# Four output additions of the shared expert ahead of the group selection, and new call orders on all five engines

## The chip, the cores and the metric

The kernel runs on one core of a Trainium2 chip. The metric is the device time of one execution in microseconds (us), the median of several runs; lower is better. The engines are TensorE (PE, its weight loads PEld), VectorE (DVE), ScalarE (ACT), GpSimd (POOL) and SyncE (SP), which issues most of the DMA.

## What is computed

```python
xn = _layernorm(x)
x = x + _L0_attn_ref(xn, Wq, Wk, Wv, Wo) + _L0_ffn_ref(xn, ...)
# attention: x is (2, 512, 512), 32 heads of 128 over 8 key heads, rope, causal
scores = jnp.einsum('bkgtd,bksd->bkgts', qg, k) * scale
attn = jax.nn.softmax(jnp.where(causal, scores, -jnp.inf), axis=-1)
out = jnp.einsum('bkgts,bksd->bkgtd', attn, v)        # then times Wo
# ffn: 16 experts in 4 groups; the best 2 groups, in them the best 2 experts
scores = softmax(xt @ router_w + router_b) + router_bias
keep = top 2 groups by their largest score; idx = top 2 experts in them
y = sum over chosen e of gate_e * (silu(xt @ w1 + b1) * (xt @ w2 + b2)) @ w3 + b3
z = silu(xt @ sw1 + sb1) * (xt @ sw2 + sb2) @ sw3 + sb3   # shared expert
```

## The kernel before

All products of weights and of attention run as three fp32r matmuls, since each operand is split into a high part and the rest (`*_hi`, `*_lo`). The high part is written by ScalarE or GpSimd (a copy to fp32r), the rest by VectorE or GpSimd (a subtraction).

**Front.** The rows are normalised, transposed, routed; the shared expert's two halves give 8 row blocks of 128 tokens each. TensorE computes `down(n)` for each block into four banks (`DOWN_BANKS`), VectorE adds it to the sum `y` (`add_down(n)`, line 1310). Four blocks are of batch 0 and four of batch 1, and `down` of one bank can only start again when VectorE has added what was in it. VectorE also does the routing: group selection (lines 1340 to 1346), then the first largest expert twice (`first_largest`, lines 1330 to 1334), `chosen`, and the gates. The key and value projection of head 0 and its queries follow on TensorE.

**Heads.** There are 8 key heads g. Head 0 is `first_head`, heads 1 to 6 run as a hardware loop over `key_head`, head 7 is `last_head`. Each of the five engines has the three functions as a plain list of calls, one per piece of work, and walks it in order; semaphores alone tie the engines together. A head holds, for each batch b and row block i: `scores` (TensorE), `maxima` (VectorE, the row maxima, line 1474), `exps` (ScalarE, line 876), `normalise` (GpSimd, line 636), `transpose_p` (TensorE), the split of the transposed probabilities (`lo_pT`, line 1502), `values` (TensorE), the split of its result (`lo_oT`, line 1487), `project_out` (TensorE) and `add_out` (VectorE). In between stand the next batch's or head's `project_kv` and `project_q`, whose results VectorE turns (`turn_k`, `turn_q1`, `turn_q2`) and GpSimd sums (`add_k`, `add_q`), and the transposition of k (`transpose_k`), whose bank must be read by `lo_kT` (line 1465) before `project_q(g, b, 2, 0)` may write it:

```python
if h < 2:
    pe.wait_ge(v_split, count(2, g, b, h + 1))
elif h == 2:
    pe.wait_ge(kT_split, count(1, g, b, 1))
```

**Experts.** Each head also carries five of the 31 expert tiles of 128 rows (`tile_of(g, m)`, 5g + m - 5; calls with a tile or head out of range do nothing). Head 0 computes the places of the rows (`first_places(0, k)` on VectorE: `count_blocks`, `first_blocks`, `row_slots`, `row_gates`, `experts_of_tiles`, lines 1370 and on) and GpSimd scatters them with indirect DMAs (`place_x`, line 645). Head 7 gathers the results (`collect`) and VectorE adds them in four steps (`combine_two(g, i)`, four instructions each on line 1586).

Of the kernel before, what the change touches and what calls it, by code (L numbers as in the profile page):

```python
# [17 lines left out]
TB = T // P  # L18
# [89 lines left out]
def build(nc, x, wq, wkv, wo, shared, sb3, w12, w3, b12, b3, router_w, router_b, router_bias,  # L108
# [8 lines left out]
    with ExitStack() as ctx:  # L117
# [167 lines left out]
        def _(sp):  # L285
# [103 lines left out]
            def first_head(g):  # L389
                e4 = load_x(tile_of(g, 4))  # L390
                load_wo(g, 1)
                e2 = load_x(tile_of(g, 2))
                load_wo(g, 3)
                e1 = load_x(tile_of(g, 1))
                e3 = load_x(tile_of(g, 3))
                load_b12(tile_of(g, 1), e1)
                load_b12(tile_of(g, 3), e3)
                load_wo(g, 2)
                load_b12(tile_of(g, 2), e2)
                load_wo(g, 0)  # L400
# [10 lines left out]
                load_wkv(g)  # L411
                load_wq(g, 1)
                store_y(tile_of(g, 0))
                store_y(tile_of(g, 3))
                load_wq(g, 2)
                load_w3(tile_of(g, 1), e1)
                load_wq(g, 3)
                load_b3(tile_of(g, 1), e1)
# [4 lines left out]
                load_b3(tile_of(g, 4), e4)  # L423
                load_b12(tile_of(g, 5), e5)
                load_w3(tile_of(g, 5), e5)
                load_b12(tile_of(g, 4), e4)
                load_b3(tile_of(g, 5), e5)
                load_w12(tile_of(g, 1), e1)

            def key_head(g):  # L430
                e1 = load_x(tile_of(g, 1))
                load_b12(tile_of(g, 1), e1)
                load_w12(tile_of(g, 1), e1)
                load_wo(g, 0)
                load_w3(tile_of(g, 1), e1)
                load_wq(g, 0)
                load_wo(g, 1)
                load_wo(g, 2)
                load_wo(g, 3)
                load_wkv(g)  # L440
                store_y(tile_of(g, 0))
                e2 = load_x(tile_of(g, 2))
                load_b3(tile_of(g, 1), e1)
                load_b12(tile_of(g, 2), e2)
                load_w12(tile_of(g, 2), e2)
                load_wq(g, 1)
                load_w3(tile_of(g, 2), e2)
                store_y(tile_of(g, 1))
                load_wq(g, 2)
                e3 = load_x(tile_of(g, 3))  # L450
                load_w12(tile_of(g, 3), e3)
                load_b3(tile_of(g, 2), e2)
                load_w3(tile_of(g, 3), e3)
                store_y(tile_of(g, 2))
                load_b12(tile_of(g, 3), e3)
                e4 = load_x(tile_of(g, 4))
                load_wq(g, 3)
                load_w12(tile_of(g, 4), e4)
                load_b3(tile_of(g, 3), e3)
                store_y(tile_of(g, 3))  # L460
                load_w3(tile_of(g, 4), e4)
                e5 = load_x(tile_of(g, 5))
                load_b12(tile_of(g, 4), e4)
                load_b3(tile_of(g, 4), e4)
                load_w12(tile_of(g, 5), e5)
                store_y(tile_of(g, 4))
                load_w3(tile_of(g, 5), e5)
                load_b12(tile_of(g, 5), e5)
                load_b3(tile_of(g, 5), e5)

            def last_head(g):
                load_wq(g, 0)
                e1 = load_x(tile_of(g, 1))
                load_wq(g, 2)
                e4 = load_x(tile_of(g, 4))
                store_y(tile_of(g, 2))
                load_w12(tile_of(g, 1), e1)
                e3 = load_x(tile_of(g, 3))
                e5 = load_x(tile_of(g, 5))
                e2 = load_x(tile_of(g, 2))  # L480
                load_wq(g, 1)
                load_b3(tile_of(g, 4), e4)
                load_w3(tile_of(g, 2), e2)
                load_b12(tile_of(g, 1), e1)
                load_b12(tile_of(g, 5), e5)
                load_b12(tile_of(g, 4), e4)
                load_wq(g, 3)
                load_b3(tile_of(g, 3), e3)
                load_wo(g, 0)
                load_w12(tile_of(g, 2), e2)  # L490
                load_wo(g, 1)
                load_w12(tile_of(g, 5), e5)
                load_b3(tile_of(g, 1), e1)
                store_y(tile_of(g, 1))
                load_b12(tile_of(g, 3), e3)
                store_y(tile_of(g, 3))
                load_wkv(g)
                load_w3(tile_of(g, 1), e1)
                load_w12(tile_of(g, 4), e4)
                load_w3(tile_of(g, 4), e4)  # L500
                load_w12(tile_of(g, 3), e3)
                store_y(tile_of(g, 0))
                load_b3(tile_of(g, 2), e2)
                load_w3(tile_of(g, 5), e5)
                load_wo(g, 3)
                store_y(tile_of(g, 4))
                load_b12(tile_of(g, 2), e2)
                load_wo(g, 2)
                load_b3(tile_of(g, 5), e5)
                load_w3(tile_of(g, 3), e3)  # L510
# [14 lines left out]
        def _(pool):  # L525
# [160 lines left out]
            def first_head(g):  # L686
# [3 lines left out]
                normalise(g, 0, 1)  # L690
                normalise(g, 0, 2)
                add_k(g, 1, 1)
                add_q(g, 1, 1)
                place_x(g, 0)
# [3 lines left out]
                collect(g, 1)  # L698
                add_q(g, 1, 3)
                split_q(g + 1, 0)  # L700
                collect(g, 2)
                split_q(g + 1, 1)
                normalise(g, 1, 0)
                collect(g, 3)
                place_x(g, 1)
                normalise(g, 1, 1)
                add_k(g + 1, 0, 0)
                place_x(g, 2)
                add_q(g + 1, 0, 0)
                add_k(g + 1, 0, 1)  # L710
                split_q(g + 1, 2)
                normalise(g, 1, 2)
# [4 lines left out]
                collect(g, 0)  # L717
                add_q(g + 1, 0, 3)

            def key_head(g):  # L720
                lo_w12(tile_of(g, 0))
                add_k(g, 1, 0)
# [3 lines left out]
                collect(g, 2)  # L726
                add_q(g, 1, 0)
                lo_w3(tile_of(g, 1))
                lo_w12(tile_of(g, 1))
                add_k(g, 1, 1)  # L730
                normalise(g, 0, 2)
                add_q(g, 1, 1)
                split_kv(g + 1)
                collect(g, 3)
                lo_w12(tile_of(g, 2))
                split_q(g + 1, 0)
# [3 lines left out]
                add_q(g, 1, 3)  # L740
                lo_w3(tile_of(g, 2))
                normalise(g, 1, 0)
                split_q(g + 1, 1)
                split_q(g + 1, 2)
                lo_w12(tile_of(g, 3))
                add_q(g + 1, 0, 0)
                collect(g, 0)
                add_k(g + 1, 0, 0)
                normalise(g, 1, 1)
                lo_w3(tile_of(g, 3))  # L750
                lo_w12(tile_of(g, 4))
                normalise(g, 1, 2)
                place_x(g, 2)
                place_x(g, 1)
                add_k(g + 1, 0, 1)
                add_q(g + 1, 0, 1)
                split_q(g + 1, 3)
                add_q(g + 1, 0, 2)
                lo_w3(tile_of(g, 4))
                normalise(g, 1, 3)  # L760
                add_q(g + 1, 0, 3)
                collect(g, 1)

            def last_head(g):
                add_k(g, 1, 0)
                lo_w3(tile_of(g, 0))
                place_x(g, 2)
                normalise(g, 0, 0)
                lo_w12(tile_of(g, 0))
                normalise(g, 0, 1)  # L770
                add_q(g, 1, 0)
                normalise(g, 0, 2)
                add_k(g, 1, 1)
                place_x(g, 1)
                add_q(g, 1, 1)
                normalise(g, 0, 3)
                add_q(g, 1, 2)
                collect(g, 0)
# [6 lines left out]
                place_x(g, 0)  # L785
                normalise(g, 1, 1)
                normalise(g, 1, 0)

# [6 lines left out]
        def _(act):  # L795
# [161 lines left out]
            def first_head(g):  # L957
                exps(g, 0, 0, 0)
                hi_wo(g, 0)
                exps(g, 0, 0, 1)  # L960
                hi_wo(g, 1)
# [249 lines left out]
        def _(dve):  # L1211
# [125 lines left out]
            for n in range(2):  # L1337
                add_down(n)
# [9 lines left out]
            for n in range(2, TB):  # L1348
                add_down(n)
# [1449 lines left out]
```

How the kernel before makes its waits and increments, by code:

```python
def wait_count(eng, sem, value):  # L51
    if not isinstance(value, int) or value > 0:
        eng.wait_ge(sem, value)
# [229 lines left out]
        @block.sync  # L284
# [18 lines left out]
            for h in range(G):  # L303
                sp.dma_start(wq_raw[:, h, :], wq[h]).then_inc(wq_in[h], 16)
            sp.dma_start(qc[:, :], q_cos).then_inc(tables_in, 16)
            sp.dma_start(qs[:, :], q_sin).then_inc(tables_in, 16)
            sp.dma_start(kr[:, :, :, :], k_rot).then_inc(tables_in, 16)
            sp.wait_ge(zeros_ok, 1)
            for n0, n1 in ZERO_PARTS:
                sp.dma_start(x_slots[P * n0:P * n1, :].rearrange("(p n) (m d) -> p (n m) d", p=P, m=2),
# [5 lines left out]
            def load_wq(g, h):  # L316
                if no_head(g + 1):
                    return
                sp.wait_ge(q_psum, count(4, g, 1, h + 1))
                sp.dma_start(wq_raw[:, h, :], row(wq, G * g + (G + h))).then_inc(wq_in[h], 16)
# [1 line left out]
            def load_wkv(g):  # L323
                if no_head(g + 1):
                    return
                sp.wait_ge(kv_psum, count(2, g, 1, 2))
                sp.dma_start(wkv_raw[:, :, :, :].rearrange("p c k o -> p (c k o)"),
                             wkv[bass.ds(g + 1, 1), :, :, :, :].rearrange("a p c k o -> (a p) (c k o)")).then_inc(wkv_in, 16)
# [1 line left out]
            def load_wo(g, c):  # L331
                if isinstance(g, int) and g == 0:
                    sp.wait_ge(down_psum, NB)
                else:
                    sp.wait_ge(o_psum, 32 * g + (c - 3))
# [873 lines left out]
        @block.vector  # L1210
# [197 lines left out]
            dve.wait_ge(tables_in, 48)
```

## Time and profile before

| | |
|---|---|
| median of 3 runs | 907.06 us (906.69 to 907.95) |
| profiled execution, its own time | 905.59 us |
| its span | 903.8 us |
| PE busy | 888.5 us, 98% of the span |
| PEld busy | 762.2 us, 84% |
| DVE busy | 677.7 us, 75% |
| ACT busy | 431.2 us, 48% |
| POOL busy | 526.5 us, 58% |
| granted TensorE clock | full in every fortieth of the span |
| moved by DMA | 97.73 MB, mean 108 GB/s |

TensorE is busy almost throughout. Its matmuls overlap, so a row's duration is longer than the distance to the next: 128x512 matmuls of one stream start 0.23 us apart. What a wait costs is therefore read as the distance between two starts less that 0.23 us. The 1.8 us between span and own time lie around the program.

### The profile page before, as it was taken

The numbers are of one execution on the slowest core, as the hardware profiler recorded it, in microseconds if no ns is written. First come the engines' busy times: TensorE is split into PE (matmuls) and PEld (weight loads), VectorE is DVE, ScalarE is ACT, GpSimd is POOL, SyncE is SP. The second block draws the span as 40 slices with busy tenths as digits, with TensorE's granted clock in tenths as the row PEclk, the third lists the DMA queues.
The fourth block names the chain that finished last, engine by engine and source line by source line (L and its number), as shares of the span: only waits on it lengthen the run. The fifth ranks groups of instructions, "written<-read, shape, count | busy, mean of one in ns | idle before, by whom it ended". The sixth has DMA issues, their size and how long they took to land.

```text
span 903.8 us, 17478 instructions
## 1 busy us (share of the span) xinstructions
PE 888.5 (98%) x5066; PEld 762.2 (84%) x5066; DVE 677.7 (75%) x1614; ACT 431.2 (48%) x1083; POOL 526.5 (58%) x638
## 2 busy tenths in 40 slices
PE   8997999999999999999999999999999999999998
PEld 7786887888888888888888889888888888888886
DVE  6688876687767876768767786768776787676886
ACT  3504543554535644454554545445453564454543
POOL 5923786565654765538554575356565476543663
PEclk9999999999999999999999999999999999999999
DMA  9910223143223532335222443224322252230242
GB/s 329 319 47 15 92 94 123 42 131 121 88 76 86 172 95 79 90 99 168 87 87 76 114 163 87 75 81 126 123 87 75 89 172 94 80 92 22 84 150 94
DMA packets 52161, 97.73 MB, mean 108 GB/s; under 512 B 5920, under 2 KB 17824, under 8 KB 52128
## 3 DMA queue, kind: packets, MB, share of 16 engines
q1 hardware_dynamic: 49568, 88.94, 31.7%
q0 software_dynamic: 2560, 8.39, 2.8%
q8 instruction: 16, 0.26, 0.1%
q14 instruction: 17, 0.14, 0.1%
HBM read 74.76 MB, written 22.54 MB: 108 GB/s over the span
## 4 chain that ended last, share of the span: by engine, by line
PE 92%; DVE 5%; issue 1%; ACT 1%; DMA 0%; POOL 0%; SPq 0%; DVEq 0%
PE bank L1992 10%; PE bank L1990 10%; PE bank L1991 10%; PE bank L2190 7%; PE bank L2129 7%; PE bank L2131 6%; PE bank L2130 6%; PE bank L2226 6%; PE bank L2222 6%; PE bank L2223 6%; PE bank L2206 4%; PE bank L2203 4%; PE bank L2204 4%; PE bank L2251 1%; PE bank L2176 1%
## 5 line engine op out<-in xcount | busy, mean ns | idle before, releaser
L636 POOL TENSOR_SCALAR prob<-prob,rsum 128x128 f32<-128x128 f32 (+3 forms) x256 | 143.9, 582 | 89.8 <-DVE rsum L1480 89.1
L876 ACT ACTIVATE prob<-bank,nmax 128x128 f32<-128x128 f32 (+3 forms) x256 | 133.7, 528 | 113.9 <-DVE nmax L1474 111.3
L1474 DVE CUSTOM_DVE_ANT_0 bank<-bank,causal 128x128 f32<-128x128 f32 (+3 forms) x256 | 122.8, 501 | 35.5 <-PE bank L1992 33.7
L1502 DVE TENSOR_TENSOR pT_lo<-bank,pT_hi 128x512 fp32r<-128x512 f32 x160 | 109.1, 684 | 29.0 <-ACT pT_hi L896 28.6
L896 ACT ACTIVATE pT_hi<-bank 128x512 fp32r<-128x512 f32 x160 | 95.0, 596 | 67.1 <-PE bank L2190 53.4
L2222 PE MATMUL bank<-wo_lo,oT_hi 128*128 128x512 f32 x256 | 106.2, 415 | 0.0
L2129 PE MATMUL bank<-xT_hi,wq_lo 128*128 128x512 f32 x256 | 104.7, 409 | 1.5 <-DVE v_lo L1458 1.4
L619 POOL TENSOR_TENSOR w_lo<-w_raw,w_hi 128x1024 fp32r<-128x1024 f32 x31 | 74.3, 2398 | 52.7 <-ACT w_hi L931 52.7
L2131 PE MATMUL bank<-xT_hi,wq_hi 128*128 128x512 f32 x256 | 101.1, 395 | 0.0
L2226 PE MATMUL bank<-wo_hi,oT_lo 128*128 128x512 f32 x256 | 100.7, 393 | 0.0
L2130 PE MATMUL bank<-xT_lo,wq_hi 128*128 128x512 f32 x256 | 100.6, 393 | 0.0
L2223 PE MATMUL bank<-wo_hi,oT_hi 128*128 128x512 f32 x256 | 100.5, 392 | 0.0
L585 POOL TENSOR_TENSOR q_first<-rot 128x128 f32<-128x128 f32 x60 | 28.3, 472 | 115.3 <-DVE rot L1430 115.1
L2190 PE MATMUL bank<-ident,prob 128*128 128x128 f32 x640 | 94.1, 272 | 0.0
L2190 PEld LDWEIGHTS bank<-ident,prob 128*128 128x128 f32 x640 | 77.7, 140 | 13.5
L1990 PE MATMUL bank<-wkv_hi,xT_lo 128*128 128x256 f32 x256 | 74.7, 292 | 1.1 <-DVE prob L1430 0.8
L1992 PE MATMUL bank<-wkv_hi,xT_hi 128*128 128x256 f32 x256 | 72.3, 282 | 0.0
L1991 PE MATMUL bank<-wkv_lo,xT_hi 128*128 128x256 f32 x256 | 71.9, 281 | 0.0
L1990 PE MATMUL bank<-kT_hi,q_lo 128*128 128x256 f32 (+2 forms) x192 | 68.0, 354 | 3.1 <-ACT prob L876 2.9
L887 ACT ACTIVATE oT_hi<-bank 128x512 fp32r<-128x512 f32 x64 | 38.1, 595 | 65.9 <-PE bank L2206 65.2
L2203 PE MATMUL bank<-pT_hi,v_lo 128*128 128x512 f32 x160 | 65.5, 409 | 0.5 <-DVE oT_lo L1487 0.5
L1991 PE MATMUL bank<-kT_lo,q_hi 128*128 128x256 f32 (+2 forms) x192 | 64.7, 337 | 0.0
(219 smaller groups left out, 2326.5 us busy)
## 6 DMA issues: line engine op xcount, KB each, us to landing
w_raw<-w SPq DMA_DIRECT2D x31, 512.0 KB, 3.5
wq_raw<-wq SPq DMA_DIRECT2D x32, 256.0 KB, 4.1
wo_raw<-wo SPq DMA_DIRECT2D x32, 256.0 KB, 2.8
xg<-x_slots SPq DMA_DIRECT2D x31, 256.0 KB, 3.5
w_raw<-w SPq DMA_DIRECT2D x31, 256.0 KB, 2.8
eb<-b SPq DMA_DIRECT2D x31, 256.0 KB, 3.9
y_slots<-eb SPq DMA_DIRECT2D x31, 256.0 KB, 2.5
x_slots<-pairs SPq DMA_DIRECT2D x3, 2048.0 KB, 16.0
```

The lines of the kernel that those rows point to most:

```text
L636: last = nc.gpsimd.tensor_scalar(row, row, rsum[:, stat(b, i, h)], 1.0, ALU.mult, ALU.mult)
L876: last = nc.scalar.activation(prob[n % 2][:, h, 0:P * (i + 1)], bank[S_BANKS[use % 2]][:, 256 * k:256 * k + P * (i + 1)], ACT.Exp, bias=nm ...
L1990: nc.tensor.matmul(dst, a_lo, c_hi, start=start and k == 0, stop=False)
L1991: nc.tensor.matmul(dst, a_hi, c_lo, start=False, stop=False)
L1992: last = nc.tensor.matmul(dst, a_hi, c_hi, start=False, stop=stop and k == len(terms) - 1)
L2129: nc.tensor.matmul(q, wq_lo[:, h, col], xT_hi[:, c, span], start=c == 0, stop=False)
L2130: nc.tensor.matmul(q, wq_hi[:, h, col], xT_lo[:, c, span], start=False, stop=False)
L2131: last = nc.tensor.matmul(q, wq_hi[:, h, col], xT_hi[:, c, span], start=False, stop=c == HC - 1)
L2190: last = nc.tensor.transpose(bank[PT_BANKS[n % 2]][:, h * P:(h + 1) * P], prob[nth(g, b, i) % 2][:, h, j * P:(j + 1) * P], ident[:, :])
L2222: nc.tensor.matmul(dst, oT_hi[:, k, h], wo_lo[:, h, :], start=h == 0, stop=False)
L2223: nc.tensor.matmul(dst, oT_hi[:, k, h], wo_hi[:, h, :], start=False, stop=False)
L2226: last = nc.tensor.matmul(dst, oT_lo[:, k, h], wo_hi[:, h, :], start=False, stop=h == G - 1)
```

## The change

Two things change. First, VectorE does the first four `add_down` ahead of the group selection, where it did two there and two behind the group masks. Second, the lists of calls `first_head`, `key_head` and `last_head` of all five engines are put in another order. Every list has the same calls for real heads and tiles as before; no instruction is added or taken away, and no tile changes its size. Behind the two removed lines all line numbers are lower by 2.

```diff
             hidden(3)
-            for n in range(2):
+            for n in range(TB):
                 add_down(n)
             in_groups = score.rearrange("p n (g e) -> p n g e", g=GROUPS)
...
             nc.vector.tensor_tensor(masked_groups, masked_groups, ...)
-            for n in range(2, TB):
-                add_down(n)
             spare, one, two = (pick[:, k] for k in range(3))
```

A line or two of the lists, from VectorE's `last_head`:

```diff
                 lo_pT(g, 1, 2, 0)
+                lo_pT(g, 1, 2, 1)
                 combine_two(g, 2)
+                lo_pT(g, 1, 2, 2)
                 inverse_sums(g, 1, 1)
-                lo_pT(g, 1, 2, 1)
-                lo_pT(g, 1, 2, 2)
                 maxima(g, 1, 0, 0)
                 maxima(g, 1, 0, 1)
                 lo_oT(g, 1, 2)
                 combine_two(g, 3)
+                lo_pT(g, 1, 1, 0)
                 inverse_sums(g, 1, 0)
-                lo_pT(g, 1, 1, 0)
                 lo_pT(g, 1, 1, 1)
```

On TensorE in `last_head`, `project_out(g, 1, 3, 0)` moves ahead of `values(g, 1, 2, 0)`, and `values(g, 1, 2, 1)` now follows that directly, where a projection, a transposition and two scores lay between. On GpSimd in `first_head`, `place_x(g, 0)` moves from behind `normalise(g, 0, 2)`, `add_k(g, 1, 1)` and `add_q(g, 1, 1)` to ahead of them, and `place_x(g, 2)` from ahead of `add_q(g + 1, 0, 0)` to behind it.

**VectorE in the front**, from the end of the shared expert's hidden rows (`hid`, `h_lo`) over the additions (line 1310) to the start of the group selection, and then the end of the group masks:

```order
 L1261 SCALAR_TENSOR_TENSOR hid<-bank,eraw,act_out 128x512
 L1265 TENSOR_TENSOR h_lo<-hid,h_hi 128x512
-L1310 TENSOR_TENSOR y<-y,bank 128x512 x2
+L1310 TENSOR_TENSOR y<-y,bank 128x512 x4
 L1340 TENSOR_REDUCE grp<-route 128x32
 L1319 TENSOR_TENSOR beat<-grp 128x128
```

The four additions stand together; the two that are gone from behind the masks stood between the last mask instruction (line 1346) and the first of `first_largest` (line 1330).

**VectorE at the start of head 0**, the maxima of row block 0 (ISA, `nmax`) and the first step of the row places (lines 1370 to 1378 before, 1368 to 1376 now). Before:

```order
L1436 TENSOR_TENSOR q_lo<-prob,q_hi 128x384
L1474 ISA bank,nmax<-bank,causal 128x128
L1474 ISA nmax 128x1
L1474 ISA bank,nmax<-bank,causal 128x128
L1474 ISA nmax 128x1
L1370 TENSOR_REDUCE iota<-before 128x16
L1371 TENSOR_SCALAR iota<-iota 128x16
L1372 TENSOR_SCALAR per_expert<-iota 128x8
L1376 TENSOR_TENSOR pairs<-bank,per_expert 128x128
L1378 TENSOR_REDUCE per_expert<-pairs 128x16
```

and now:

```order
L1434 TENSOR_TENSOR q_lo<-prob,q_hi 128x384
L1368 TENSOR_REDUCE iota<-before 128x16
L1369 TENSOR_SCALAR iota<-iota 128x16
L1370 TENSOR_SCALAR per_expert<-iota 128x8
L1374 TENSOR_TENSOR pairs<-bank,per_expert 128x128
L1376 TENSOR_REDUCE per_expert<-pairs 128x16
L1472 ISA bank,nmax<-bank,causal 128x128
L1472 ISA nmax 128x1
```

`count_blocks`, the five instructions on 128x16 and the like, has moved from behind the first `maxima` call to ahead of it.

**VectorE in the loop**, in batch 0's last scores of each head, where `wo_lo` is `lo_wo(g, 2)`, `h_rows` the end of `expert_hidden`, and `kT_lo` is `lo_kT(g, 1)`. Before:

```order
L1562 SCALAR_TENSOR_TENSOR h_rows<-sig,gated 128x128
L1470 REGISTER_ALU
L1474 ISA bank,nmax<-bank,causal 128x512
L1474 ISA nmax 128x1
L1527 TENSOR_TENSOR wo_lo<-wo_raw,wo_hi 128x512
L1464 ISA
L1465 TENSOR_TENSOR kT_lo<-bank,kT_hi 128x512
```

and now:

```order
L1525 TENSOR_TENSOR wo_lo<-wo_raw,wo_hi 128x512
L1560 SCALAR_TENSOR_TENSOR h_rows<-sig,gated 128x128
L1468 REGISTER_ALU
L1472 ISA bank,nmax<-bank,causal 128x512
L1472 ISA nmax 128x1
L1462 ISA
L1463 TENSOR_TENSOR kT_lo<-bank,kT_hi 128x512
```

The subtraction of `wo_lo` has moved from directly ahead of `kT_lo` to ahead of `h_rows` and the maxima.

## Rows read from the trace of the kernel before

**Rows 1.** Busy time in stretches: stretch, length, each engine's busy us, PE clock, DMA

```profile
70.00:92.00 22.00, 17.44 (x121) 14.59 (x120) 18.37 (x62) 10.64 (x31) 9.23 (x15) 1.00 0.12 37
...
271.00:378.00 107.00, 107.00 (x625) 93.07 (x624) 80.05 (x193) 54.12 (x137) 62.45 (x74) 1.00 0.34 104
...
860.00:904.00 44.00, 39.65 (x206) 31.79 (x204) 34.43 (x75) 17.33 (x48) 21.14 (x28) 1.00 0.40 120
```

**Rows 2.** Waits of PE: line, released by, us in total, times, longest

```profile
PE bank L1990 <- ACT prob L876: 2.9, 4, 1.0
...
PE bank L2129 <- DVE v_lo L1458: 1.4, 2, 1.1
...
PE bank L2206 <- DVE pT_lo L1502: 0.5, 2, 0.4
```

**Rows 3.** Timeline of PE in the front: start, duration, idle before and releaser

```profile
48.57 0.40 PE L1992 MATMUL bank<-ew_hi,h_hi 128*128 128x512 f32 x1
49.96 0.50 PE L1990 MATMUL bank<-ew_hi,h_lo 128*128 128x512 f32 x1 [0.98 <-DVE y L1310]
```

**Rows 4.** Timeline of DVE, the additions and the turning of q

```profile
49.22 1.28 DVE L1310 TENSOR_TENSOR y<-y,bank 128x512 f32<-128x512 f32 x2
...
61.60 0.69 DVE L1422 TENSOR_TENSOR rot<-bank,qc 128x512 f32<-128x512 f32 x1 [1.09 <-PE bank L2131]
```

**Rows 5.** Timeline of DVE at the start of head 0

```profile
76.31 0.41 DVE L1370 TENSOR_REDUCE iota<-before 128x16 f32<-128x256 f32 x1
...
78.00 0.30 DVE L1474 CUSTOM_DVE_ANT_0 bank<-bank,causal 128x128 f32<-128x128 f32 x1 [0.23 <-DVE per_expert L1378]
```

**Rows 6.** Timeline of ACT at the start of head 0

```profile
75.36 1.28 ACT L876 ACT_TABLE_LOAD   x1
76.65 0.37 ACT L876 ACTIVATE prob<-bank,nmax 128x128 f32<-128x128 f32 x1
```

**Rows 7.** Timeline of POOL, PE and DVE in head 0, 129 to 144 us

```profile
129.34 0.97 POOL L645 DMA_INDIRECT x_slots<-xn,slots  x1 [0.30 <-issue]
130.04 0.34 PE L1992 MATMUL bank<-kT_hi,q_hi 128*128 128x384 f32 x1
...
131.56 0.57 DVE L1474 CUSTOM_DVE_ANT_0 bank<-bank,causal 128x384 f32<-128x384 f32 x1 [2.21 <-PE bank L1992]
...
143.45 0.48 PE L2129 MATMUL bank<-xT_hi,wq_lo 128*128 128x512 f32 x1 [1.11 <-DVE v_lo L1458]
```

**Rows 8.** Waits of PEld in the loop, 164 to 806 us

```profile
PEld bank L2129 <- DVE kT_lo L1465: 2.7, 6, 0.5
```

**Rows 9.** Timeline of all engines around `kT_lo` in the first loop head

```profile
202.14 1.01 DVE L1527 TENSOR_TENSOR wo_lo<-wo_raw,wo_hi 128x512 fp32r<-128x512 f32 x1
...
202.58 1.06 POOL L545 TENSOR_SCALAR wkv_hi<-wkv_raw 128x512 fp32r<-128x512 f32 x1
...
203.08 0.68 DVE L1465 TENSOR_TENSOR kT_lo<-bank,kT_hi 128x512 fp32r<-128x512 f32 x1
...
203.31 0.40 PE L2226 MATMUL bank<-wo_hi,oT_lo 128*128 128x512 f32 x1
...
203.81 0.50 PE L2129 MATMUL bank<-xT_hi,wq_lo 128*128 128x512 f32 x1
```

**Rows 10.** Line 1527: count, duration ns least/median/most, first and last start

```profile
L1527 DVE TENSOR_TENSOR wo_lo<-wo_raw,wo_hi x32: 673/684/1011, 92.8 to 853.9; 128x512 fp32r<-128x512 f32 x32
```

**Rows 11.** Timeline of PE in head 0, transpositions of k and the next q matmul

```profile
149.80 0.60 PE L2159 MATMUL bank<-ident,ksum 128*128 128x128 f32 x4
...
152.07 0.47 PE L2129 MATMUL bank<-xT_hi,wq_lo 128*128 128x512 f32 x1
```

**Rows 12.** Timeline of DVE and PE in head 7, a combining step and what follows

```profile
888.12 3.12 DVE L1586 SCALAR_TENSOR_TENSOR y<-gath,slot_gate,y 128x512 f32<-128x512 f32 x4
...
891.34 0.39 PE L2204 MATMUL bank<-pT_hi,v_hi 128*128 128x512 f32 x1
...
892.08 0.50 PE L2206 MATMUL bank<-pT_lo,v_hi 128*128 128x512 f32 x1 [0.35 <-DVE pT_lo L1502]
```

More of the change, by code:

```diff
@@ L2310, in first_head @@
                 scores(g, 0, 3, 1)
-                scores(g, 0, 3, 2)
                 project_q(g, 1, 1, 3)
                 project_out(g, 0, 0, 0)
-                values(g, 0, 1, 0)
+                scores(g, 0, 3, 2)
                 scores(g, 0, 3, 3)
@@ L2665, in last_head @@
                 transpose_p(g, 0, 3, 3)
+                scores(g, 1, 1, 0)
+                transpose_h(tile_of(g, 2))
                 values(g, 0, 3, 1)
+                scores(g, 1, 1, 1)
+                project_out(g, 0, 2, 1)
+                values(g, 0, 3, 2)
+                transpose_p(g, 1, 0, 0)
+                expert_down(tile_of(g, 2))
+                project_q(g + 1, 0, 0, 0)
+                values(g, 0, 3, 3)
+                project_q(g + 1, 0, 0, 1)
+                transpose_x(tile_of(g, 3))
@@ new lines, in key_head @@
+                project_out(g, 0, 2, 2)
+                project_q(g + 1, 0, 0, 2)
+                scores(g, 1, 2, 0)
+                project_q(g + 1, 0, 0, 3)
+                first_ranks(g)
+                project_out(g, 0, 2, 3)
+                scores(g, 1, 2, 1)
+                expert_up(tile_of(g, 3))
+                project_kv(g + 1, 0, 1, 0)
+                scores(g, 1, 2, 2)
+                scores(g, 1, 2, 3)
+                project_kv(g + 1, 0, 1, 1)
+                project_out(g, 0, 3, 0)
@@ new lines, in key_head @@
+                project_out(g, 0, 3, 1)
+                values(g, 1, 0, 0)
+                transpose_p(g, 1, 1, 0)
+                project_out(g, 0, 3, 2)
+                transpose_p(g, 1, 1, 1)
+                project_out(g, 0, 3, 3)
+                scores(g, 1, 3, 0)
+                transpose_h(tile_of(g, 3))
+                project_q(g + 1, 0, 1, 0)
+                scores(g, 1, 3, 1)
+                project_q(g + 1, 0, 1, 1)
+                project_out(g, 1, 0, 0)
+                scores(g, 1, 3, 2)
@@ new lines, in key_head @@
+                project_q(g + 1, 0, 1, 2)
+                project_q(g + 1, 0, 1, 3)
+                project_out(g, 1, 0, 1)
+                expert_down(tile_of(g, 3))
+                values(g, 1, 1, 0)
+                project_out(g, 1, 0, 2)
+                transpose_p(g, 1, 2, 0)
+                transpose_k(g + 1, 0)
+                scores(g, 1, 3, 3)
+                transpose_x(tile_of(g, 4))
+                project_out(g, 1, 0, 3)
+                project_q(g + 1, 0, 2, 0)
+                values(g, 1, 1, 1)
```

1515 lines of the change are left out of this document (733 added, 782 removed).

## The prediction

> **What bounds the kernel now.** I read the busy time by stretches first. In a head of the loop TensorE is busy for the whole 107.00 us at full clock, VectorE for 80, ScalarE for 54, GpSimd for 62, and the DMA share is a third [rows 1]. So TensorE's stream is the bound, the change neither adds nor removes a matmul, and all that an order can give is TensorE's waiting. The ends have some of that: from 70 to 92 us TensorE is busy 17.44 of 22.00, and from 860 to 904 us 39.65 of 44.00, where the last additions and the last store behind the final matmul take most of the rest [rows 1]. Second I read the list of TensorE's waits: the dearest that an order could touch are four for the exponentials, 2.9 us in all, two for `v_lo`, 1.4 us, and two for `pT_lo`, 0.5 us [rows 2]. The front's wait for an addition is in the timeline [rows 3]. Third, since a busy mark hides short gaps of a pipelined engine, I read the waits of the weight loads in the loop: six for `kT_lo`, 0.5 us each [rows 8], once per head and found in no matmul's idle time. There is nothing large: everything together is some 7 us, and each term below is at most 1.8.
>
> **The change part by part.** The sum is made against the profiled execution's own 905.59 us, which is 1.47 below the median shown, 907.06; I carry that difference over at the end.
>
> *The additions, front.* `down` of the seventh block starts at 49.96 where its predecessor started at 48.57, and the stream's pitch is 0.23: 49.96 - 48.57 - 0.23 = 1.16 us lost. The bank is free only once the third addition is done, and that stands behind the whole group selection, at 49.22 [rows 3, 4]. With four additions together the last is done some 4 x 0.64 = 2.6 us (two take 1.28) behind the start of the first, well before 48.57. The group selection starts 1.3 us later and ends where it ends now, because two additions are gone from its end: its chain stays as it is. The question is whether the 1.16 us reach the later work. The turning of the first queries starts at 61.60 after 1.09 us of waiting for TensorE [rows 4], so VectorE has that much room there. Term: -1.1 us, bounds -1.16 and 0 (if the routing chain alone set the start of head 0).
>
> *The first step of the row places, head 0.* `count_blocks` takes from 76.31 to 78.00, 1.69 us [rows 5], and now stands ahead of the first maxima, which were done at 76.31. Their exponential ran at 76.65, right behind the table load [rows 6], and would now come behind 78.0. The next maxima, which started at 78.00, move only by the 0.5 us or so of the call put between. TensorE already waits for exponentials in this stretch (the four waits of [rows 2] are mostly here), so each delay goes straight into its stream until the queries' projection, which takes one further wait away from it. I get 0.3 us on the second use, 0.4 to 0.5 on the later ones. Term: +0.5 us; bounds 0, and 78.0 - 76.65 = 1.35.
>
> The rows give the load as 1.28 us and the next activation 1.29 us behind its start. The Trainium skill, "ScalarE: Activation LUTs", What ACT_TABLE_LOAD costs, puts a drain of about 1380 ns on top, 2.66 us in all. By that page the exponential could not start before about 78.0 in either order, and putting `count_blocks` first would be free, the whole sum then 0.5 us lower; the row contradicts it here, since the activation starts at 76.65, and the sum goes by the row.
>
> *Row scatters, head 0.* Two results of TensorE are taken up late while GpSimd issues indirect DMAs: matmuls that started at 130.04 and take 0.34 are followed by the maxima at 131.56, 1.2 us late, and a `v_lo` later on costs TensorE 1.11 us at 143.45 [rows 7]. One of the four waits for exponentials follows from the first (2.9 / 4, some 0.7 us). What makes the signal late the rows don't say; it happens beside the scatters and not in every one. The scatters of blocks 0 and 1 move ahead of three calls, the last ones behind one, so other matmuls end beside them. I take -0.5 us, as if one of the two waits were missed half of the time more than one is found anew; bounds -1.8 (both gone) and +1.0 (one more).
>
> *The loop.* In each head `project_q(g, 1, 2, 0)` starts 203.81 - 203.31 = 0.50 behind its predecessor, 0.27 more than the pitch, and its weight load had waited for `kT_lo` [rows 8, 9]. `kT_lo` stands behind `wo_lo`, which here takes 1.01 us against 0.684 in the median [rows 9, 10], while GpSimd writes to SBUF beside it [rows 9]. With `wo_lo` ahead of `expert_hidden` and the maxima, `kT_lo` can start at about 202.2 and end at 202.9. TensorE has one 0.23 us matmul group fewer between the transposition and that projection by the order, about 0.4 us, so it wants `kT_lo` at 203.1: enough. The gain is 6 x 0.27 = 1.6 us at most. I take -1.2, since the many other calls that moved may put back a short gap; bounds -1.6 and 0.
>
> *The last head.* `values` at 892.08 starts 0.74 behind its predecessor, 0.51 more than the pitch, for a `pT_lo` that stands behind a 3.12 us combining step [rows 12]. The other `pT_lo` wait [rows 2] is 0.5 - 0.35 = 0.15 of idle, and with the same 0.16 for the restart 0.3. In the new lists one `pT_lo` more stands ahead of each of the last two combining steps. TensorE then asks for the second `pT_lo` earlier, so a piece of the gain at 892 may be paid at the step before. Term: -0.9 (both, and a little where a restart is saved in the same way); bounds -1.2 and 0.
>
> Sum: -1.1 + 0.5 - 0.5 - 1.2 - 0.9 = -3.2 us, 902.4 by its own time. With 1.47 for the median: **903.9 us**, 0.35% faster. A measurement of this kernel can tell about 0.2%, 1.8 us, from no change, so the border of faster is 905.25, that of slower 908.87.
>
> **The rivals.**
>
> *It comes out the same (0.24).* The front's 1.1 us is real, but head 0 is short of exponentials and eats it: +1.35 at the first places, the scatters' late signals as they are, and the loop's wait replaced by another of the same size, since in 107 us of new order any call may come just too early. -1.1 + 1.35 + 0 - 0.5 (loop) - 0.5 (last head) = -0.75: 906.3. For it: 98% busy leaves nothing that a reordering surely wins. Against it: the loop's wait has a plain cause that is plainly moved.
>
> *A new wait in the loop, slower (0.14).* Everything there counts six times. The tightest spot that I find by the order is `kT_lo(g + 1, 0)`: between the transpositions of k and the q matmul that waits for it TensorE's starts will now lie about 2.3 us apart, where by the order it was 3.0. In head 0 the same pair lay 152.07 - 149.80 = 2.3 apart and ran without a wait [rows 11]; but there VectorE had nothing else to do, and now an addition and a maxima call stand ahead. If these are just behind, each head loses up to their 0.7 + 0.7 us. It decides from 0.64 us per head, since (1.8 + 3.2 - 1.2) / 6 = 0.64; at 0.8 the loop adds 4.8 in place of its -1.2, and the sum is -2.0 + 4.8 = +2.8: 909.9. Against it: DVE is busy 80 of 107, and a late call catches up at once.
>
> *More than I take (in the likeliest case's lower part).* Both late signals gone and no loss at the first places: -1.1 - 1.8 - 1.6 - 1.2 = -5.7, 901.4.
>
> *The orders do nothing, only the additions count* lies in the first rival: -1.1, 906.0.
>
> **How the numbers follow.** Likeliest case 0.62, 903.9, its own range 902.0 to 905.3: its ends are one of the larger bounds (the scatters' or the loop's) going the other way. Same 0.24, 905.3 to 907.8. Slower 0.14, 908.9 to 912. The range 902.0 to 908.2 leaves out about 0.05 below and 0.13 above. Faster by over 0.2% 0.61, within 0.25, slower 0.14.
>
> **What would show it.** In the new profile: the gap ahead of the seventh block's `down`, at about 48.8, is gone and the first scores start 1.1 us earlier. The exponential behind the table load starts near 78 instead of 76.65, at unchanged length of the load. The list of weight-load waits in the loop has no `kT_lo`, and the distance between two heads is 0.27 us shorter; a longer one tells of the slower rival, and the row of waits names its call. GpSimd's scatters have late takers or not, to be read as idle time of VectorE ahead of `maxima` or `krot` of over 1 us behind a finished matmul. In the last head the `pT_lo` waits are gone. The forecast is wrong above all if the exponentials of head 0 hold up TensorE by more than 1 us in sum, or if a loop head grows.

## The result: slower by 1.6%, and the profile after

The changed kernel takes 921.68 us in the median of 4 runs (918.85 to 924.25), the kernel before 907.23 us beside it: a ratio of 1.0158, interval 1.0124 to 1.0192, 14.5 us slower. The prediction said 903.9, in a range of 902.0 to 908.2. The profiled execution took 924.25 us at a span of 922.5, so the sums below, which are made against it and the 903.8 us span of before, have 18.7 us to find.

Busy time by stretches of the changed kernel, columns as in [rows 1]:

```profile
70.00:92.00 22.00, 18.89 (x124) 16.69 (x125) 18.88 (x64) 10.38 (x31) 10.23 (x16) 0.92 0.11 39
...
271.00:378.00 107.00, 104.91 (x609) 89.30 (x608) 82.25 (x188) 52.45 (x134) 59.62 (x71) 1.00 0.32 104
```

TensorE's waits over the whole kernel, and then the weight loads' waits in the loop (164 to 806 us), columns as in [rows 2] and [rows 8]:

```profile
PE bank L2249 <- DVE eb L1576: 5.0, 6, 0.9
PE bank L2267 <- DVE h_rows L1560: 3.8, 6, 1.1
PE bank L1988 <- ACT prob L876: 2.6, 3, 1.0
...
PE bank L2157 <- POOL ksum L593: 2.4, 4, 0.8
PE bank L2220 <- DVE wo_lo L1525: 1.4, 1, 1.4
...
PEld bank L2249 <- issue: 7.4, 6, 1.3
...
PEld bank L2157 <- DVE rot L1428: 4.6, 6, 1.2
...
PEld bank L2127 <- DVE kT_lo L1463: 0.9, 5, 0.2
```

In this stretch of the loop TensorE was busy throughout; now it misses 2.1 us of busy time in 107. Of TensorE's waits three lie in the loop and come about once per head (those for `prob` and `wo_lo` lie in the first and the last head): the four transpositions of the next tile's rows wait for the addition `eb`, the transposition of `h_rows` waits for VectorE, and `transpose_k` waits for GpSimd's `ksum`. The wait for `kT_lo` of [rows 8], 0.5 us each, is down to 0.2. The wait for `v_lo` of [rows 2] is gone.

The length of a head is read from `transpose_k(g, 1)`, the same call in the second and the third loop head of the changed kernel:

```profile
310.57 0.63 PE L2157 MATMUL bank<-ident,ksum 128*128 128x128 f32 x4 [0.82 <-POOL ksum L593]
...
420.81 0.63 PE L2157 MATMUL bank<-ident,ksum 128*128 128x128 f32 x4 [0.56 <-POOL ksum L593]
```

That is 110.24 us. In the kernel with only the additions moved, whose loop is that of before, it is 413.27 - 306.01 = 107.26. So this head is 2.98 us longer. The heads are not all alike: the five distances between the six loop heads sum to 550.72 us against 536.87, a mean of 2.77 us more, so six heads cost some 16.6 us in this execution.

Then SyncE's queue, ScalarE, VectorE and GpSimd at the place where the delay begins:

```profile
286.17 0.34 SPq L356 DMA_DIRECT2D w_raw<-w  x1
296.08 0.95 SPq L337 DMA_DIRECT2D wo_raw<-wo  x2
297.22 0.33 SPq L363 DMA_DIRECT2D eb<-b  x1
297.74 0.33 SPq L371 DMA_DIRECT2D w_raw<-w  x1
298.32 0.33 SPq L337 DMA_DIRECT2D wo_raw<-wo  x1
...
304.11 0.63 ACT L914 ACTIVATE wo_hi<-wo_raw 128x512 fp32r<-128x512 f32 x1 [2.13 <-DMA wo_raw<-wo]
304.65 0.58 ACT L922 ACTIVATE xgT_hi<-bank 128x512 fp32r<-128x512 f32 x1
...
305.26 0.69 DVE L1533 TENSOR_TENSOR xgT_lo<-bank,xgT_hi 128x512 fp32r<-128x512 f32 x1 [2.15 <-ACT xgT_hi L922]
...
306.84 2.89 POOL L636 TENSOR_SCALAR prob<-prob,rsum 128x384 f32<-128x384 f32 x4 [6.22 <-DVE rsum L1478]
...
307.00 0.68 DVE L1525 TENSOR_TENSOR wo_lo<-wo_raw,wo_hi 128x512 fp32r<-128x512 f32 x1
```

`load_wo(g, 2)` stands third in SyncE's list and must wait until the old third quarter of `wo` has been used, so that SyncE issues nothing for 9.9 us; the quarter that ScalarE needs first, `load_wo(g, 0)`, stands behind it, behind another quarter and two further loads, and is issued only at 298.32 in a burst. ScalarE waits 2.13 us for it with `xgT_hi` queued behind, and VectorE waits 2.15 us for that. Behind `xgT_lo` on VectorE stand the reciprocals `rsum`, for which GpSimd waits 6.22 us before it can normalise; only behind the four `prob` instructions (2.89 us) comes its `ksum`. So TensorE stands at `transpose_k`, and then at `h_rows`, which comes later on VectorE for the same reason.

And VectorE a little later in the same head, with GpSimd beside it:

```profile
316.35 2.60 POOL L619 TENSOR_TENSOR w_lo<-w_raw,w_hi 128x1024 fp32r<-128x1024 f32 x1
...
317.22 2.29 DVE L1525 TENSOR_TENSOR wo_lo<-wo_raw,wo_hi 128x512 fp32r<-128x512 f32 x1
...
319.52 0.65 DVE L1576 TENSOR_TENSOR eb<-eb,bank 128x512 f32<-128x512 f32 x1
...
320.31 0.63 PE L2249 MATMUL bank<-ident,xg 128*128 128x128 f32 x4 [0.76 <-DVE eb L1576]
```

This `wo_lo` is `lo_wo(g, 3)`, the last quarter, not the third one that the prediction looked at. 0.684 us in the median before [rows 10], it takes 2.29 us while GpSimd subtracts in SBUF too, and the addition `eb` that TensorE waits for stands behind it.

### The profile page after: what moved, and what is told of

Its sections match the earlier page's. It is cut to its first block, busy times and chain, and to the rows that moved or that the text cites. A ratio compares the mean times of both kernels' runs of the same rounds, so it can differ in the third digit from the quotient of the medians.

```text
span 922.5 us, 17497 instructions
## 1 busy us (share of the span) xinstructions
PE 896.5 (97%) x5066; PEld 758.6 (82%) x5066; DVE 704.4 (76%) x1614; ACT 430.1 (47%) x1083; POOL 524.4 (57%) x638
## 4 chain that ended last, share of the span: by engine, by line
PE 72%; DVE 12%; issue 7%; DMA 4%; ACT 2%; SPq 1%; DVEq 0%; POOL 0%; another core or an unknown queue 0%; ACTq 0%; POOLq 0%
PE bank L1988 8%; PE bank L1990 8%; PE bank L1989 8%; PE bank L2224 6%; PE bank L2188 5%; PE bank L2220 5%; PE bank L2221 5%; PE bank L2127 4%; PE bank L2129 4%; PE bank L2128 4%; DMA wo_raw<-wo 3%; PE bank L2204 3%; PE bank L2201 3%; PE bank L2202 3%; DVE wo_lo L1525 2%
## 5 line engine op out<-in xcount | busy, mean ns | idle before, releaser
L2201 PE MATMUL bank<-pT_hi,v_lo 128*128 128x512 f32 x160 | 68.2, 426 | 0.0
L1990 PE MATMUL bank<-kT_hi,q_hi 128*128 128x256 f32 (+2 forms) x192 | 64.7, 337 | 0.0
```

What stands on the lines that cost most here:

```text
L1990: last = nc.tensor.matmul(dst, a_hi, c_hi, start=False, stop=stop and k == len(terms) - 1)
```

## The experiments

Each time stands beside runs of the kernel before on the same chip. Those medians lay between 906.71 and 907.05. The lengths of a head below are those between `transpose_k(g, 1)` of the second and the third loop head.

**Only the additions.** The kernel before with the code edit and no new order:

```diff
-            for n in range(2):
+            for n in range(TB):
                 add_down(n)
...
-            for n in range(2, TB):
-                add_down(n)
```

> The kernel before with only the four additions ahead of the group selection; all call orders as before. If the front's gain is real and reaches the end, the wait of 0.98 us ahead of the seventh block's down is gone and the time is 1.1 us lower than before (906.0). If the first head's routing chain or its exponentials set the pace, the time stays within 0.3 us of before.

Measured: 905.08 us beside 906.71, ratio 0.9982 (0.9972 to 0.9991), 1.6 us faster. The wait of [rows 3] is gone from the trace. The gain is real and reaches the end; 1.1 us lies inside its interval.

**The loop's orders taken back.** The changed kernel with the five `key_head` lists of before; of VectorE's:

```diff
             def key_head(g):
...
-                lo_wo(g, 2)
                 expert_hidden(tile_of(g, 1))
                 maxima(g, 0, 3, 2)
+                lo_wo(g, 2)
                 lo_kT(g, 1)
...
```

> The changed kernel with the six loop heads' call orders of before on all five engines; the additions, the first head and the last head stay changed. If the loop alone carries the loss, a loop head takes 107.3 us again (110.3 in the changed kernel) and the time falls from 921.7 by about 6 x 3.0 = 18 us, to 903 to 906, and tells what the parts outside the loop are worth. If the first or last head hands delays on, it stays above 909.

Measured: 905.73 us beside 906.71, ratio 0.9992 (0.9983 to 1.0001). The loop carries the loss, 15.1 us by the two ratios; what lies outside it, additions included, is worth about 1 us.

**SyncE's list of the loop taken back.** The changed kernel with SyncE's `key_head` of before, which begins:

```diff
             def key_head(g):
                 e1 = load_x(tile_of(g, 1))
-                load_w12(tile_of(g, 1), e1)
-                load_wo(g, 2)
-                load_wo(g, 1)
                 load_b12(tile_of(g, 1), e1)
-                load_w3(tile_of(g, 1), e1)
+                load_w12(tile_of(g, 1), e1)
                 load_wo(g, 0)
-                store_y(tile_of(g, 0))
+                load_w3(tile_of(g, 1), e1)
+                load_wq(g, 0)
+                load_wo(g, 1)
+                load_wo(g, 2)
                 load_wo(g, 3)
...
```

> The changed kernel with only SyncE's list of the loop head from before, so that the first quarter of wo is asked for first and as soon as it may be. Theory of the late load: in the changed kernel that quarter is issued behind the third and second and lands about 2 us after ScalarE asks for it; with it early the wait of ScalarE for wo_raw (2.1 us) and TensorE's waits for ksum and h_rows (0.8 and 0.66 per head) go, and the time is about 6 x 2 = 12 us lower, 908 to 911. Rival, contention of GpSimd with VectorE's subtractions: the time falls by less than 3 us.

Measured: 911.8 us, ratio 1.0061 (1.0044 to 1.0078): 9.9 us less than the changed kernel by the medians, 8.8 by the ratios, so most of the 14.5 hangs on one engine's list of loads. That is at the upper end of what the theory allowed (908 to 911), and this list is no clean test of the late load: TensorE's waits for `ksum` and `h_rows` are gone and that for `eb` is nearly gone (0.6 us in all), but a new one stands in their place, for `oT_lo`, 5.8 us over the six heads.

GpSimd's list of before in the loop of the changed kernel has no time: with the other engines' new lists it deadlocks, the engines waiting for one another. So the share of GpSimd's new order is not measured by itself.

**One exchange in that list.**

```diff
-                load_wo(g, 2)
+                load_wo(g, 0)
                 load_wo(g, 1)
                 load_b12(tile_of(g, 1), e1)
                 load_w3(tile_of(g, 1), e1)
-                load_wo(g, 0)
+                load_wo(g, 2)
```

> The changed kernel with one exchange in SyncE's list of the loop head: load_wo(g, 0) and load_wo(g, 2) change places, nothing else. Theory of the late load: the order of these two is what made the kernel slow, so this takes back as much as SyncE's whole list of before did (911.8 against 921.7): 909 to 913, and ScalarE's wait of 2.1 us for wo_raw in each head is gone. If it was another of SyncE's calls, it stays at 918 or more.

Measured: 910.52 us, ratio 1.0041 (1.0026 to 1.0055), 11 us under the changed kernel by the exchange of two lines. ScalarE's wait for `wo_raw` is not among its waits in the loop any more, TensorE's waits for `ksum` and `h_rows` went with it, and the head is 108.67 us long, 1.57 less:

```profile
306.01 0.60 PE L2157 MATMUL bank<-ident,ksum 128*128 128x128 f32 x4
...
414.68 0.60 PE L2157 MATMUL bank<-ident,ksum 128*128 128x128 f32 x4
...
PE bank L2249 <- DVE eb L1576: 3.6, 6, 0.6
```

What stays is the wait for `eb`.

**GpSimd's subtraction cut.** This kernel leaves out the low part of `w1` and `w2`; TensorE has as many matmuls as before.

```diff
-nc.gpsimd.tensor_tensor(w12_lo[:, :, :], w12_raw[:, :, :], w12_hi[:, :, :].bitcast(F32), ALU.subtract)
+nc.gpsimd.tensor_tensor(w12_lo[:, 0, 0:32], w12_raw[:, 0, 0:32], w12_hi[:, 0, 0:32].bitcast(F32), ALU.subtract)
...
-[(xgT_hi[:, c, :], xgT_lo[:, c, :], w12_hi[:, c, :], w12_lo[:, c, :])
+[(xgT_hi[:, c, :], xgT_lo[:, c, :], w12_hi[:, c, :], w12_hi[:, c, :])
```

> The changed kernel with GpSimd's subtraction for the low part of w1 and w2 cut to 32 columns in all expert tiles, and the high part read in its place by TensorE (the low part of these weights is left out). It takes 2.4 us of two-input SBUF work per tile off GpSimd and nothing off VectorE. Theory of contention as a cause of its own: VectorE's wo_lo falls from 1.11 to about 0.7 us in the mean and q_lo from 0.87 to 0.6, TensorE's wait of 5.0 us for the eb addition goes, and the time falls by 6 us or more. Theory of the late load alone: it falls by less than 3 us, since ScalarE still waits for wo_raw.

Measured: 915.84 us, ratio 1.0091 (1.0074 to 1.0107), 5.8 us under the changed kernel, just short of the 6 that was asked for. The wait for `eb` is gone, `wo_lo` is at 0.72 us in the mean; `q_lo` stays at 0.85, so it meets other work of GpSimd. ScalarE still waits for `wo_raw` in each head.

**Both.** On top of the changed kernel, the two edits last shown:

```diff
-                load_wo(g, 2)
+                load_wo(g, 0)
...
-nc.gpsimd.tensor_tensor(w12_lo[:, :, :], w12_raw[:, :, :], w12_hi[:, :, :].bitcast(F32), ALU.subtract)
+nc.gpsimd.tensor_tensor(w12_lo[:, 0, 0:32], w12_raw[:, 0, 0:32], w12_hi[:, 0, 0:32].bitcast(F32), ALU.subtract)
```

> Both edits together: the exchange of the two loads, and GpSimd's low part of w1 and w2 cut (left out). If the late load and the contention together are the whole loss of the loop, a head takes 107.0 to 107.4 us, as before, and the time is 903 to 906. If a head still takes over 108, a third cause is left, the order on VectorE or ScalarE.

Measured: 905.3 us, ratio 0.9987 (0.9978 to 0.9996). A head of the loop, from 305.23 to 412.73 by the same call, takes 107.50 us, 0.1 above what was expected of two causes alone. `lo_wo(g, 2)` ahead of `expert_hidden` is still in this kernel, so in these surroundings it costs little. This kernel has less to compute than the changed one on GpSimd, so it says what the contention costs, not what a better order would reach.

**The prediction's own edit, by itself.** On top of the additions:

```diff
+                lo_wo(g, 2)
                 expert_hidden(tile_of(g, 1))
                 maxima(g, 0, 3, 2)
-                lo_wo(g, 2)
                 lo_kT(g, 1)
```

> The kernel before with the four additions ahead, and in VectorE's loop head lo_wo(g, 2) moved ahead of expert_hidden, as in the changed kernel; all other orders as before. The prediction's term: the wait for kT_lo, 0.24 us per head, goes, so the time is 1.4 us under that of the additions alone (905.1): 903.7. Rival: the subtraction only moves its delay to h_rows and to the maxima behind it, and the time is the same or higher.

Measured: 911.46 us, ratio 1.0059 (1.0043 to 1.0075), against 0.9982 for the additions alone: 7 us slower where 1.4 less was forecast. VectorE, GpSimd and TensorE in the third loop head:

```profile
415.10 1.09 DVE L1525 TENSOR_TENSOR wo_lo<-wo_raw,wo_hi 128x512 fp32r<-128x512 f32 x1
415.74 1.58 POOL L547 TENSOR_TENSOR wkv_lo<-wkv_raw,wkv_hi 128x512 fp32r<-128x512 f32 x1
416.12 1.35 DVE L1560 SCALAR_TENSOR_TENSOR h_rows<-sig,gated 128x128 f32<-128x128 f32 x1
...
417.52 0.33 PE L2267 MATMUL bank<-ident,h_rows 128*128 128x128 f32 x1 [1.23 <-DVE h_rows L1560]
```

`wo_lo` takes its 1.1 us all the same, and it pushes `h_rows`, which reads SBUF alone and takes 0.28 us undisturbed, into GpSimd's `wkv_lo`: 1.35 us. A head is 108.46 us long, 1.2 more than with the additions alone. TensorE now waits 1.23 us per head for `h_rows` where it had lost 0.27 for `kT_lo`.

**The first head's orders.** On top of the additions, all five `first_head` lists of the changed kernel; of VectorE's:

```diff
-                maxima(g, 0, 0, 0)
                 first_places(g, 0)
+                maxima(g, 0, 0, 0)
                 maxima(g, 0, 0, 1)
...
```

> The kernel before with the four additions ahead, and the first head's call orders of the changed kernel on all five engines; loop and last head as before. In the traces the first head takes 91.4 us in the new orders and 93.1 in the old, but the first loop head behind it 108.7 against 107.6, since its first row transposition and additions meet other neighbours. Theory: net 0.5 to 0.6 us below the additions alone, 904.4 beside a before of 906.9. Rival: the gain of the first head is real but all given back, and the time is that of the additions alone, 905.1.

Measured: 903.52 us beside 907.05, ratio 0.9962 (0.9948 to 0.9975), the fastest kernel here, 3.5 us under before and 1.8 of it from the first head by the two ratios. That part is small: the two intervals just touch, and the profiled executions have spans of 902.8 us here and 902.6 with the additions alone. In them `transpose_k(g, 1)` of the first loop head comes 1.5 us earlier (197.14 against 198.63), and the distance from there to the second is 1.3 us longer (108.65 against 107.38), where the old loop's orders meet the new first head.

**The last head's orders.** On top of the additions, all five `last_head` lists; of VectorE's:

```diff
                 lo_pT(g, 1, 2, 0)
-                combine_two(g, 2)
-                inverse_sums(g, 1, 1)
+                expert_product(tile_of(g, 2))
                 lo_pT(g, 1, 2, 1)
-                expert_product(tile_of(g, 3))
+                combine_two(g, 2)
...
```

> The kernel before with the four additions ahead, and the last head's call orders of the changed kernel on all five engines. The prediction's term: the waits for pT_lo behind the combining steps go, 0.9 us under the additions alone. What the traces of the changed kernels show speaks against it: the waits go, but six new gaps of 0.15 to 0.37 us stand in their place, and 1.4 us are lost where the old loop order meets the new last head: 1 to 2 us above the additions alone, 906 to 907.

Measured: 907.78 us, ratio 1.0004 (0.9995 to 1.0013), 2.0 us slower than the additions alone by the two ratios. The two waits for `pT_lo` behind the combining steps are gone as said, but a new one of 0.61 us stands at 862.35, and shorter gaps beside it. Where the old loop meets the new last head TensorE waits 1.30 us for an addition (`y`, at 813.43); yet the distance from the last loop head's `transpose_k(g, 1)` to the last head's is no longer than with the additions alone, 105.78 us against 105.83. From there to the end it is 63.47 against 61.30: the 2 us are lost in the second half of the last head.

**The subtraction behind the addition.** On top of the exchange of the loads:

```diff
-                lo_wo(g, 3)
                 inverse_sums(g, 0, 3)
                 add_b3(tile_of(g, 1))
+                lo_wo(g, 3)
```

> The changed kernel with the exchange of the two loads of wo, and in VectorE's loop head lo_wo(g, 3) moved from ahead of inverse_sums and add_b3 to behind them. Theory: that subtraction of two SBUF operands takes 2.29 us beside GpSimd's split of w, and the addition that TensorE waits for 0.85 us per head stands behind it; with the addition ahead the wait goes and the time is about 5 us under that of the exchange alone (910.5): 905 to 906. Rival: the subtraction holds up the low part of the probabilities or the turning of q instead, and the time falls by less than 1.5 us.

Measured: 906.87 us, ratio 0.9998 (0.9988 to 1.0007), 3.9 us under the exchange alone by the two ratios. That is a little above the 905 to 906 expected. The wait for `eb` is gone, `wo_lo` is at 0.80 us in the mean of the loop and `q_lo` still at 0.85. Two moves, of a load and of a subtraction, take the changed kernel back to the time of before.

**The late load in the old orders.** On top of the additions, `load_wo(g, 0)` and `load_wo(g, 2)` exchanged in SyncE's loop list.

> The kernel before with the four additions ahead and, in SyncE's loop head, load_wo(g, 0) and load_wo(g, 2) exchanged, so that the first quarter of wo is asked for where the third stood. If the late load is a cause by itself, ScalarE waits for wo_raw in each head and the time rises from 905.1 by 6 us or more. If it hurts only with the other new orders around it, it rises by less than 2 us.

Measured: 971.16 us, ratio 1.0708 (1.0661 to 1.0756), 66 us slower. The two lines do far more harm here. `load_w3` and `load_wq` are queued behind the load that has to wait:

```profile
413.64 0.33 SPq L356 DMA_DIRECT2D w_raw<-w  x1
432.46 0.33 SPq L337 DMA_DIRECT2D wo_raw<-wo  x1
432.97 0.33 SPq L371 DMA_DIRECT2D w_raw<-w  x1
...
435.59 0.63 ACT L939 ACTIVATE w_hi<-w_raw 128x512 fp32r<-128x512 f32 x1 [6.89 <-DMA w_raw<-w]
...
441.05 0.79 PE L2127 MATMUL bank<-xT_hi,wq_lo 128*128 128x512 f32 x1 [8.11 <-DVE v_lo L1456]
```

SyncE issues nothing for 18.8 us, where it was 9.9 in the changed kernel; ScalarE waits for the weights that stood behind, and TensorE for `v_lo` behind those, 52.7 us over the six heads. The mean granted clock of this execution is 0.97, so a part of the 66 us is the clock's. Why the same exchange holds the queue up for longer in these orders was not taken apart.

**`kT_lo` ahead of `wo_lo`.** On top of the additions and the first head:

```diff
                 maxima(g, 0, 3, 2)
-                lo_wo(g, 2)
                 lo_kT(g, 1)
+                lo_wo(g, 2)
                 lo_q(g, 1, 1)
```

> The four additions ahead, the first head's orders of the changed kernel, the loop and the last head as before, and in VectorE's loop head lo_kT(g, 1) ahead of lo_wo(g, 2), where they stood the other way round. Nothing but that subtraction of wo changes its place, and nobody waits for it soon. Theory: kT_lo starts 0.9 us earlier, TensorE's gap of 0.25 us per head ahead of project_q(g, 1, 2, 0) goes and nothing is queued later, so the time is 1 to 1.5 us under that of the additions and first head (903.5): 902.3. Rival, drawn from the run with the subtraction ahead of expert_hidden: behind lo_kT it meets GpSimd's split of wkv for longer and delays the low part of q or the maxima, and the time stays or rises.

Measured: 908.2 us beside 906.72, ratio 1.002 (1.001 to 1.003), against 0.9962 without the exchange: 5 us slower.

```profile
415.25 0.91 DVE L1525 TENSOR_TENSOR wo_lo<-wo_raw,wo_hi 128x512 fp32r<-128x512 f32 x1
416.08 1.64 DVE L1434 TENSOR_TENSOR q_lo<-rot,q_hi 128x384 fp32r<-128x384 f32 x1
...
419.28 0.47 PE L1988 MATMUL bank<-w_hi,hT_lo 128*128 128x512 f32 x1 [0.98 <-DVE hT_lo L1567]
```

The wait for `kT_lo` is gone, and `q_lo`, 0.55 us undisturbed, takes 1.64 beside `wkv_lo`; everything behind it is late, and TensorE waits 0.98 us for `hT_lo`. The rival was right.

## Why the prediction was wrong

**What bounds it: right.** TensorE's stream is the bound before, and the loss of the loop shows as TensorE's waiting.

**The additions, -1.1: right.** Alone they gave -1.6, interval -2.5 to -0.8.

**The first step of the row places, +0.5: about right.** ScalarE in the changed kernel, and TensorE's waits at this place with the additions and the first head, and with the additions alone (both at full clock):

```profile
74.69 1.28 ACT L876 ACT_TABLE_LOAD   x1
77.51 0.37 ACT L876 ACTIVATE prob<-bank,nmax 128x128 f32<-128x128 f32 x1 [1.54 <-DVE nmax L1472]
...
78.56 0.37 ACT L876 ACTIVATE prob<-bank,nmax 128x128 f32<-128x128 f32 x1
```

```profile
77.95 0.35 PE L1988 MATMUL bank<-kT_hi,q_lo 128*128 128x256 f32 x1 [2.16 <-ACT prob L876]
```

```profile
76.20 0.36 PE L1988 MATMUL bank<-kT_hi,q_lo 128*128 128x256 f32 x1 [0.63 <-ACT prob L876]
78.19 0.35 PE L1988 MATMUL bank<-kT_hi,q_lo 128*128 128x256 f32 x1 [1.05 <-ACT prob L876]
```

The first exponential starts 2.8 us behind the start of the table load where it was 1.29 [rows 6], as late as said, but the four now follow one another at once. One wait of 2.16 us stands where there were two of 1.68 in sum, and the queries' projection behind them starts 0.3 us later (79.71 against 79.42).

**The row scatters, -0.5: the size was off, towards its bound of -1.8.** The first head as a whole gave -1.8 us by the ratios. With the additions alone TensorE still waits 0.79 us for an exponential at 131.70 and 0.66 for a `v_lo`; with the first head's new orders it waits for neither. This split is read from traces, not from a run of each, and the first loop head gave 1.3 us of it back.

**The loop, -1.2 with bounds -1.6 and 0: this step failed.** It measured +15.1 by the run with the loop's orders taken back, +16.6 by the distances between the heads. The part on `kT_lo` was right in that its wait went down, from 0.5 to 0.2 us. Wrong was to book that as the whole effect, with 0 as the worst.

The bound of 0 left out SyncE's list altogether: nothing was worked out for the loads, though `load_wo(g, 2)` has to wait for the last but one projection of the head before and `load_wo(g, 0)` now stands behind it. It also left out the other calls of VectorE that moved: `lo_wo(g, 3)` now falls beside GpSimd's `w_lo`, ahead of an addition that TensorE waits for. Of the 2.98 us per head, 110.24 - 108.67 = 1.57 are that load, 108.67 - 107.50 = 1.17 the contention with one instruction of GpSimd, and 107.50 - 107.26 = 0.24 other places. By the means of the five distances, 110.14, 108.52, 107.60 and 107.37 us, it is 1.62, 0.92 and 0.23.

The prediction's own edit was mis-sized too, though it is not what made the changed kernel slow. The prediction's own row had this subtraction at 1.01 us beside GpSimd's instruction [rows 9, 10], and it took the call as costing nothing where it went to; the two edits that move it alone, by two calls and by one, each made the kernel 5 to 7 us slower. In the changed kernel, where everything around it moved as well, the same call takes 0.83 us and `h_rows` behind it is not slowed:

```profile
311.65 0.83 DVE L1525 TENSOR_TENSOR wo_lo<-wo_raw,wo_hi 128x512 fp32r<-128x512 f32 x1
312.41 0.28 DVE L1560 SCALAR_TENSOR_TENSOR h_rows<-sig,gated 128x128 f32<-128x128 f32 x1
```

VectorE was taken as having 27 us per head to spare [rows 1]; what counts is which instruction that reads only SBUF falls beside GpSimd's, and who waits behind it.

**The last head, -0.9: wrong in sign.** Measured +2.0 by itself. The two `pT_lo` waits went, but one of 0.61 us came, and the starts of `project_out` and `values` matmuls that now stand closer together lie 0.1 to 0.4 us further apart in several places; that they wait for each other's results is likely and was not tested. In the new loop's surroundings a part comes back: with both edits together the distance to the last head's `transpose_k(g, 1)` is 104.28 us instead of 105.83, and from there to the end it is 63.34. In the changed kernel the last head holds one larger loss that no step named:

```profile
867.62 3.97 DVE L1525 TENSOR_TENSOR wo_lo<-wo_raw,wo_hi 128x512 fp32r<-128x512 f32 x1
868.35 2.70 POOL L636 TENSOR_SCALAR prob<-prob,rsum 128x512 f32<-128x512 f32 x4
...
871.65 0.50 PE L2220 MATMUL bank<-wo_lo,oT_hi 128*128 128x512 f32 x1 [1.35 <-DVE wo_lo L1525]
```

**The slower rival, 0.14,** was of the right kind, a wait in the loop that counts six times, and at the wrong place: it named `kT_lo(g + 1, 0)`, which nobody waits for long. Its chance was too low: the argument against it, "a late call catches up at once", holds for VectorE's average and not for a chain that runs from a load over four engines.

Open stays what makes TensorE's results late beside the row scatters, and which of the last head's calls cost it its 2 us; neither was taken apart.

## What to carry to other kernels

When call lists are laid out anew, walk the queue of the loads as strictly as the compute engines: a load that must wait for its buffer holds every load behind it, so buffers go in the order in which they come free and the first one needed stands first. Price an instruction of VectorE that reads only SBUF by its row beside GpSimd's work, and look at where it lands as well as at what it leaves; moving one such call by one place cost 5 us here. In this kernel, whose bound engine was full, a reordering of the loop had 0.27 us per head to win by the prediction's own row, and lost nearly three.

## What the hardware showed that was not expected

VectorE's groups in the loop (164 to 806 us), line, shapes, count, busy us and mean ns, first of the changed kernel, then two of before:

```profile
L1500 DVE TENSOR_TENSOR pT_lo<-bank,pT_hi 128x512 fp32r<-128x512 f32 x117 | 80.2, 685 | 21.9 <-ACT pT_hi L896 21.3
L1434 DVE TENSOR_TENSOR q_lo<-rot,q_hi 128x384 fp32r<-128x384 f32 x46 | 40.3, 875 | 9.0 <-ACT q_hi L853 9.0
L1525 DVE TENSOR_TENSOR wo_lo<-wo_raw,wo_hi 128x512 fp32r<-128x512 f32 x24 | 26.6, 1110 | 0.0
```

```profile
L1436 DVE TENSOR_TENSOR q_lo<-rot,q_hi 128x384 fp32r<-128x384 f32 x48 | 28.4, 591 | 1.2 <-ACT q_hi L853 0.7
L1527 DVE TENSOR_TENSOR wo_lo<-wo_raw,wo_hi 128x512 fp32r<-128x512 f32 x24 | 17.5, 748 | 0.0
```

A subtraction that reads one operand from PSUM (`pT_lo`) takes 685 ns in the loop whatever the order; one of the same size with both operands in SBUF takes 0.68 us alone, 2.29 us beside GpSimd's `w_lo`, and 3.97 us beside the end of GpSimd's `rot` sum and its four `prob` instructions, which have one tensor operand each. At 3.97 us it began 0.7 us before the four, while `rot` ran, and ended 0.5 us behind their end: it hardly ran while GpSimd did. But it isn't always VectorE that stands. The `wo_lo` at 307.00 ran wholly beside the first of GpSimd's four `prob` and took its 0.68 us; there it was that `prob` that took 1.21 us, against 0.58 for each of the three behind it. What decides which of the two goes first no run here shows, so that beside GpSimd a subtraction can be slowed, and need not be. The Trainium skill, "GPSIMD Engine Reference", section 8 (Key points), says that GpSimd shares its SBUF interfaces with VectorE and contends with its instructions that have two SBUF inputs. The traces agree, in either direction: the two-operand subtractions grow up to sixfold or GpSimd's instruction grows in their place, and the subtraction with a PSUM operand does not grow.

In the profiled execution of the changed kernel the granted clock fell to half, the 1.2 GHz level, for some 3 us of the first head, behind a stretch in which TensorE was busy half of the time; before, it was full throughout. Two of the four runs had a full clock at 921.3 and 918.6 us of span, so the result does not rest on it.

```profile
71.00:72.00 1.00, 0.49 (x17) 0.39 (x14) 0.99 (x2) 0.48 (x1) 0.00 (x0) 1.00 0.07 16
...
74.00:76.00 2.00, 2.00 (x12) 2.00 (x11) 1.23 (x4) 1.80 (x2) 0.11 (x1) 0.54 0.00 0
```
